# Second feed-forward of a two-layer gated transformer block: the order of two chains of small instructions on GpSimd

## The reference, cut to what matters

```
def rms_norm(x, g):
    var = jnp.mean(x * x, axis=-1, keepdims=True)
    return x * jax.lax.rsqrt(var + EPS) * g
def activation_quant(x):
    scale = 127.0 / jnp.clip(jnp.max(jnp.abs(x), axis=-1, keepdims=True), 1e-05, None)
    return jnp.clip(jnp.round(x * scale), -128, 127) / scale
def bit_linear(x, w, g):              # w is rounded to -1, 0, 1 times one scale
    xn = rms_norm(x, g)
    xq = ste(xn, activation_quant(xn))
    wq = ste(w, weight_quant(w))
    return xq @ wq.T
y = bit_linear(x, gate_w, gate_norm_w)          # 512 -> 2 * 1408
gate, up = jnp.split(y, 2, axis=-1)
h = gate * jax.nn.sigmoid(gate) * up
return bit_linear(h, down_w, down_norm_w)       # 1408 -> 512
x = x + jnp.tanh(g_ffn[1]) * _L1_ffn_ref(_layernorm(x, axis=-1), ...)
```

## Time and profile before

| | us |
|---|---|
| median of 3 runs | 825.64 (823.56 to 826.14) |
| the profiled execution, its own time | 826.4 |
| its span (first to last instruction) | 824.6 |
| around the span | 1.8 |
| stage of the change, from the start of `ffn1` on PE to the end | 656 to 824.6 |

### The profile page before, as it was taken

The page is one execution under the profiler, slowest core; times in us unless marked ns, Lnnn a source line. Parts: engine busy times, 40 slices in busy tenths (PEclk is TensorE's granted clock), DMA queues, the critical chain, the costliest instruction groups (busy, mean ns, idle before and its releaser), DMA issues. The chain is left out here.

```text
span 824.6 us, 13670 instructions
## 1 busy us (share of the span) xinstructions
PE 666.3 (81%) x5174; PEld 363.6 (44%) x5174; DVE 640.6 (78%) x978; ACT 608.6 (74%) x813; POOL 387.7 (47%) x494
## 2 busy tenths in 40 slices
PE   8863367875966876779989996999999799888886
PEld 6431123332422433445654663556645444444443
DVE  3689999899999898887885678656635458888884
ACT  3787699899779896488883787479937437677775
POOL 1116526557695866364383156311303426555552
PEclk9986589799879998689999999999999899999999
DMA  8900310000000000622231021121300100000001
GB/s 312 395 3 0 122 31 2 0 1 1 1 0 2 0 1 1 230 71 72 90 115 36 2 72 40 44 72 53 103 1 2 36 1 14 26 27 27 31 35 51
DMA packets 21905, 43.72 MB, mean 53 GB/s; under 512 B 3920, under 2 KB 8528, under 8 KB 21072
## 3 DMA queue, kind: packets, MB, share of 16 engines
q1 hardware_dynamic: 21840, 42.85, 15.1%
HBM read 38.61 MB, written 4.19 MB: 52 GB/s over the span
## 5 line engine op out<-in xcount | busy, mean ns | idle before, releaser
L1740 DVE TENSOR_REDUCE c_nmax<-c_s 128x1 f32<-128x384 f32 (+3 forms) x176 | 108.5, 632 | 80.4 <-PE c_s L1957 80.3
L1857 ACT ACTIVATE c_probs<-c_e 128x512 f32<-128x512 f32 (+1 forms) x176 | 94.5, 559 | 52.2 <-PE c_e L1987 51.1
L1665 POOL TENSOR_TENSOR c_psum<-c_probs 128x1536 f32<-128x1536 f32 x16 | 56.7, 3543 | 134.0 <-ACT c_probs L1857 134.0
L1418 PE MATMUL b_y<-w2q,b_q2T 128*128 128x512 bf16 x256 | 74.3, 444 | 41.5 <-ACT b_q2T L1318 20.5
L2306 PE MATMUL d_gu<-gateq,d_xqT 128*128 128x512 bf16 (+1 forms) x384 | 84.0, 362 | 14.0 <-ACT d_xqT L2231 13.7
L1954 PE MATMUL c_s<-c_kT,c_qaT 96*128 96x128 f16 (+3 forms) x256 | 72.1, 314 | 21.6 <-DVE c_nmax L1740 20.2
L1389 PE MATMUL b_up<-shared,b_xqT 128*128 128x512 bf16 x256 | 73.0, 411 | 2.5 <-ACT hidden L1284 2.5
L1985 PE MATMUL c_e<-c_qaT,c_kT 98*128 98x512 f16 (+3 forms) x256 | 68.9, 303 | 3.5 <-ACT c_qaT L1844 3.0
L1418 PEld LDWEIGHTS b_y<-w2q,b_q2T 128*128 128x128 bf16 x256 | 26.3, 109 | 80.2 <-issue 35.4
L2306 PEld LDWEIGHTS d_gu<-gateq,d_xqT 128*128 128x128 bf16 x384 | 35.1, 98 | 50.3 <-ACT d_xqT L2231 19.7
L1954 PEld LDWEIGHTS c_s<-c_kT,c_qaT 96*128 96x128 f16 x256 | 25.3, 100 | 67.1 <-DVE c_nmax L1740 44.7
(11 more groups left out here) (245 smaller groups left out, 1874.1 us busy)
## 6 DMA issues: line engine op xcount, KB each, us to landing
c_stage<-in_gateT SPq DMA_DIRECT2D x16, 704.0 KB, 4.0
c_stage<-in_downT SPq DMA_DIRECT2D x6, 768.0 KB, 4.4
xs<-in_x SPq DMA_DIRECT2D x4, 1024.0 KB, 14.6
a_w1f<-in_w1T SPq DMA_DIRECT2D x2, 2048.0 KB, 16.9
hidden<-in_w2T SPq DMA_DIRECT2D x2, 2048.0 KB, 21.6
out<-xs SPq DMA_DIRECT2D x16, 256.0 KB, 2.0
b_ln_g<-in_ln_g SPq DMA_DIRECT2D x1, 1024.0 KB, 4.8
b_ln_b<-in_ln_b SPq DMA_DIRECT2D x1, 1024.0 KB, 8.4
```

What stands on the lines that cost most here:

```text
L1418: last = nc.tensor.matmul(y_ps[:], q2T[:, n % 2, c, :], w2q[:, c, :], start=(c == 0), stop=(c == IC - 1))
L1665: nc.gpsimd.tensor_tensor(psum[:], region(slot, 0)[:, :, P:], region(slot, 1), ALU.add).then_inc(psum_ready, 1)
L1740: nc.vector.tensor_reduce(nmax[:, G % 2, i, n:n + heads], s_ps[u % 2][:, 0:heads * (i + 1) * P].rearrange("p (n k) -> p n k", n=heads), ax ...
L1857: nc.scalar.activation(probs[:, G % 2, at:at + width], e_ps[fill % 3][:, 0:width], ACT.Exp).then_inc(e_read, 1)
```

## The change

In POOL's loop the two calls of a turn change places: the factors of the input two tiles ahead come first, the scale of the last intermediate second.

```
             for n in range(TOTAL + 1):
+                inputs.scales(pool, n + 2)
                 scales(n - 1)
-                inputs.scales(pool, n + 2)
```

## The result

| | before | after |
|---|---|---|
| median | 824.74 us (823.56 to 826.14, 6 runs) | 907.12 us (905.57 to 908.72, 6 runs) |
| ratio to before | | 1.0987 (95% interval 1.0971 to 1.1003) |
| the profiled execution, its own time | 826.4 us | 906.24 us |
| its span | 824.6 us | 904.4 us |

The change made the kernel 9.9% slower: the medians are 82.4 us apart, the two profiled executions 79.8. The forecast was 906 us.

The account below looks back on a forecast made before the run. The prediction took a circle of waits through DVE, POOL and ACT, 9.26 us a turn, as the bound; 826.4 + 60.2 (longer circle) + 20.4 (TensorE's clock) = 907.0, predicted as 906 us, range 894 to 918.

Parts of the forecast that it names:

- The input chain: POOL's L275 to L283: held up only by DVE, so moving it forward gains 0 in the steady part.
- The moved chain: POOL's L2205 to L2215: now behind L283, it and the ACT work behind it add 4.63 us a turn, 60.2 in all.
- the circle: Waits from DVE's L267 through POOL's L283 and ACT's L290 back to DVE's L2145: 9.26 us a turn, the bound.
- ACT's idle 2.42 us before L290: ACT's wait for L283: it cannot hide the new work, which comes after L283.
- The clock: TensorE falls to 1.2 GHz in the longer idle gap: 1.7 us a turn in 12 turns, 20.4 us.
- rival B: TensorE's clock stays at 2.4 GHz, so only the longer circle costs: 886 us; chance 8%.
- POOL's hold by DVE: POOL's L281 beside DVE's L2157: stays at 1.17 us, change taken as 0, ends -11.7 and +7.5 us.
- The sum: Whole kernel: 826.4 + 60.2 + 20.4 = 907.0 us against the profiled execution, 906 predicted.
- C: TensorE stays at 1.2 GHz through the stage and becomes the bound, turns at least 16.28 us: 917 us; chance 6%.
- D: The hold of POOL by DVE's L2157 shifts, with the clock falling: 894 or 914 us; chance 7%.
- E: Not slower: the factor is there when ACT reaches L2257: 814 to 826 us; chance 3%.
- DVE's branch: DVE's path from the start of L2257 to the next L2145: 4.35 us, hidden behind ACT's 4.63 by 0.3.

Follow-up runs that it names:

- e1: The kernel before, with the two POOL calls exchanged in turn 7 alone: 831.89 us, ratio 1.0071.
- e2: The changed kernel, with 36 unread matmuls on TensorE ahead of its wait for the rounded intermediate in turns 2 to 14: 887.27 us, ratio 1.0737.
- e5: The changed kernel, with both readers of the moved chain (ACT's rounding, PE's transposes) put later: 844.06 us, ratio 1.0203.
- e6: The kernel before, old POOL order, with ACT's rounding of the intermediate and PE's transposes put later: 845.52 us, ratio 1.0228.
- e3: The kernel before, with one more small power instruction in POOL's chain for the last intermediate, every turn: 826.92 us, ratio 1.0006.
- e4: The changed kernel, with one more small power instruction in POOL's chain for the last intermediate: 917.33 us, ratio 1.1101.
- e8: The kernel before, with ACT's squares of the intermediate put ahead of its rounding of the input: 813.86 us, ratio 0.9847.
- e10: The kernel before, with POOL's L281 put behind L283 and given its own semaphore: 820.44 us, ratio 0.9939.

## Why the prediction was right, point by point

- *The input chain gains nothing by going first.* Right. L278 waits 0.48 us for DVE before and after.
- *The moved chain and its readers enter the circle at 4.63 us a turn.* Right. The first changed turn is 13.89 us as forecast, e1's is 13.87, and with the clock kept up (e2) they are 13.86. e5 and e6 show that it is the readers' places that carry this cost, e3 and e4 that the chain is in the circle after the change and outside it before.
- *ACT's idle 2.42 us before L290 is no cover for work that comes after L283.* Right. The same idle time is a cover for the squares in e8 and for the dose in e3, since both come before L290 without needing L283.
- *The clock, 12 x 1.7 = 20.4 us.* Right, with the size off by little and the count by one. Between the first and the last L290 it is 12 x (15.53 - 13.89) = 19.7. But 13 gaps brought 1.2 GHz, not 12: the last one delays what comes behind the last L290, and that makes the 1.13 us by which the end grew (in e2, with the clock up, the end is 27.9 us as before). The prediction left this out; in the profiled execution the earlier first L290 (1.26 us) hides it. The bounds were 0 and 1.92; e1 shows 1.89 for one turn, and the slowest turns of the changed kernel have 15.76 - 13.89 = 1.87. The others are shorter, down to 15.05, as the clock came back during the eight matmuls. e2 shows the term on the chip: with the gap filled the kernel is at 887, which is the time worked out for rival B to within 1.5 us.
- *POOL's hold by DVE stays as it was.* Right in the steady turns (1.17). In two early turns L280 was held (2.05 and 1.77 us), as in the kernel before (2.04 twice). e10 shows that the hold goes with the place, e5 and e6 that it grows to 1.73 us when the place shifts.
- *The sum.* 80.6 us forecast on the profiled execution, 79.8 measured.
- *The rivals.* B's condition, a clock that stays up, did not hold; C did not either, since PE stood idle 4.5 to 5.3 us in every changed turn; D did not; E did not, as L2257 waited 6.1 to 7.8 us for its factor.
- *DVE's branch is hidden by 0.3 us, PE's at the full clock by 0.13.* Hidden, yes, but DVE's by less: in e2, where the clock stays up, DVE's L2145 waits only 0.17 us for ACT in its turn. ACT does not wait for PE there. No run lengthened DVE's branch.

## What to carry to other kernels

In a pipeline whose turn is longer than the work of each of its engines, find the circle of waits that closes after one turn, and ask of every moved instruction whether its *readers* stand ahead of the circle's next step in some engine's list; one small instruction more in a chain tells it at once (0 us in the old order, 0.62 us a turn in the new). Idle time on an engine can hide only work that does not need what ends the wait. And when a wait grows on TensorE, count its clock as a separate term: here it was a quarter of the whole loss.

## What the runs showed of the hardware that was not expected

Adding work made a kernel faster, which e2 was built to try: 36 matmuls of 256 columns a turn, read by nobody, brought the changed kernel from 907.1 to 887.3 us, because the granted clock stayed at 2.4 GHz when the idle gap on TensorE was 1.35 us instead of 5.28.

GpSimd's hold beside VectorE's L2157 depends on a few hundredths of a microsecond of timing. POOL's L280 took 0.56 us when it started 0.07 us ahead of L2157 (757.43 and 757.50), and 2.04 when the two started together (692.02). The hold falls on whichever instruction is there: L281 or, moved, L283 took 1.17 us instead of 0.27. It is no simple rule of who comes first: in e5 L281 started 0.05 us ahead of L2157 and was held all the same.
